# Expert outputs scattered to token order by GpSimd and read back with plain loads, and a re-timed first half of the second sequence's latent attention

## The chip, the cores and the metric

One core of a Trainium2 chip runs the whole kernel. The metric is the device time of one execution in microseconds (us). Before the change the median of three executions is 2420.44 us (2420.27 to 2422.87). Five engines work beside each other: PE (TensorE, matrix products), DVE (VectorE), ACT (ScalarE), POOL (GpSimd) and SP (SyncE, here only an issuer of DMAs). They meet through semaphores.

## The reference

`x` is 2 x 1024 x 256, seen as 2048 rows of 256 floats. Six residual steps follow each other; each reads a layer norm of all that came before:

```python
x = x + 0.5 * moe(norm(x))        # 16 experts, top 2, 256 -> 512 -> 256
x = x + causal_attention(norm(x)) # 16 heads of 16
x = x + 0.5 * moe(norm(x))        # the same weights again
x = x + 0.5 * lora(norm(x))       # base product + 8 routed low-rank pairs, top 2
x = x + latent_attention(norm(x)) # 16 heads, latents of 48 and 64, rotary 64, no mask
x = x + 0.5 * lora(norm(x))
# moe:  out += combine[:, e:e+1] * (silu(x @ W1[e]) @ W2[e])  for 16 experts,
#       combine = softmax of the top 2 router logits at their experts, 0 elsewhere
```

## The kernel before

`X` stays in on-chip memory as 16 token tiles, each 128 rows of 256 floats. Stages run one after the other, each a block in which every engine has its own program; between blocks all engines meet at a barrier.

**Expert stage** (`moe_stage`, run twice). DVE normalizes the token tiles and works out the router's top two. For every token POOL scatters its normalized row twice (L575, 64 indirect DMAs in the two runs) to a slot list in HBM, `slots_in`, grouped by expert; the unused tails of each expert's list are zeroed by plain DMAs from a tile of zeros (L311, on ACT's and SP's queues). Then 48 expert tiles of 128 slots are worked through, two per turn of a loop: SP loads a tile (L328, L329), PE turns it (L539), multiplies it with the first weights (L550), ACT applies SiLU (L473), PE turns and multiplies again (L556, L564), ACT copies the result to `YS` (L477) and stores it in slot order to `slots_out` (L479). `PO` holds for each token the two slots that its outputs went to, and `GH` the two gate weights.

**Reading the outputs** (`ExpertSums`). The stage that follows an expert stage (attention after the first, lora after the second) begins by gathering: per token tile POOL issues two indirect DMAs by `PO` (L218, L219), 32 of them a stage, and DVE adds the two gathered rows, weighted, to `X` and takes the row statistics (L227, L230, L233, L236; `add`). ACT takes the roots (L148), and DVE normalizes (L160). In attention, ACT first writes constants into `att_QT` and `att_KT` (L1038, L1039), then copies and rounds what PE turns and projects (L790, L815; L974, L988). In lora SP also loads the latent stage's big weights ahead (L1236, L1237).

**Latent stage** (`mla_stage`). Two sequences of 1024 rows, each with eight pairs of heads; a pair is 16 steps `s`. Each step has scores on PE (L1752), exponentials on ACT (L1930) and value products on PE (L1761), with sums of exponentials on POOL (L1654). A row's maximum is taken from rough scores (L1733) that PE computes in pieces and DVE reduces (L2062), one pair ahead. In the last pair of the first sequence (`after` in the code) each step also carries a share of the second sequence's front: turning the normalized rows (`xn_transposes`, L1673), the down projection (L1683), the latents' norm (`latent_scales`, L2023 to L2028), their transposes (L1690) and the first rotary projections (L1708, L2042 to L2056). Behind it stand eight turns of the up projection (L1781), each followed by three pieces of the next pair's rough scores.

Of the kernel before, what the change touches and what calls it, by code (L numbers as in the profile page):

```python
# [41 lines left out]
ROWS = NT * P + P  # L42
NB4 = 4
# [20 lines left out]
MOE_STEPS = 55  # L64
# [99 lines left out]
def load_stage(nc, g, dram):  # L164
# [3 lines left out]
    s_z = g.sem("zeros_made")  # L168
    s_zd = g.sem("zero_tile_stored")
    with nc.Block() as block:  # L170
        @block.sync
        def _(sp):
            g.credit(sp)
            sp.dma_start(g.X[:, :, :], dram["x"].rearrange("(t p) d -> p t d", p=P)).then_inc(s_in.handle, 16)
            sp.dma_start(g.C[:, :], dram["const"]).then_inc(s_c.handle, 16)
            sp.wait_ge(s_z.handle, s_z.at(1))
            sp.dma_start(g.XG[NE * ROWS:NE * ROWS + P, :], g.Z[:, :]).then_inc(s_zd.handle, 16)
            sp.wait_ge(s_zd.handle, s_zd.at(16))
            sp.wait_ge(s_c.handle, s_c.at(16))

        @block.vector
        def _(dve):
            dve.memset(g.Z[:, :], 0.0).then_inc(s_z.handle, 1)
# [6 lines left out]
class ExpertSums:  # L190


    NQ = 8
    PER = NT // NQ

    def __init__(self, g, rep):
        S = lambda name, each, **kind: g.sem("moe_" + name, each, rep, **kind)
        self.g = g
        self.s_po, self.s_yd = S("out_rows", 1), S("expert_out_stored", 16 * NTILE)
        self.s_ga = [S(f"rows_gathered{q}", 32 * self.PER, pool_dma=True) for q in range(self.NQ)]  # L200
# [8 lines left out]
    def gather(self, pool, tiles):  # L209

        g, s_second = self.g, self.s_second
        pool.wait_ge(self.s_po.handle, self.s_po.at(1))
        pool.wait_ge(self.s_yd.handle, self.s_yd.at(16 * NTILE))
        for t in tiles:
            if t >= NT // 2:
                pool.wait_ge(s_second.handle, s_second.at(t - NT // 2 + 1))
            s_ga = self.s_ga[t // self.PER]
            pool.indirect_dma_start(self.Y1[:, t, :], None, g.YG, bass.IndirectOffsetOnAxis(g.PO[:, 0, t:t + 1], 0)).then_inc(s_ga.handle, 16)  # L218
            pool.indirect_dma_start(self.Y2[:, t % (NT // 2), :], None, g.YG, bass.IndirectOffsetOnAxis(g.PO[:, 1, t:t + 1], 0)).then_inc(s_ga.handle, 16)  # L219

    def add(self, dve, q, s_mv):

        g = self.g
        tiles = range(q * self.PER, (q + 1) * self.PER)
        dve.wait_ge(self.s_ga[q].handle, self.s_ga[q].at(32 * self.PER))
# [13 lines left out]
def moe_stage(nc, g, dram, rep):  # L239
# [16 lines left out]
    s_pos, s_ei, s_ri, s_po = S("slots", NB4), S("tile_experts", 1), S("tile_rows", 1), S("out_rows", 1)  # L256
    s_tz, s_zt = S("tail_rows", 1), S("tails_zeroed", 16 * NE)
# [6 lines left out]
    s_yd = S("expert_out_stored", 16 * NTILE)  # L264
# [4 lines left out]
    with ExitStack() as ctx:  # L269
# [16 lines left out]
        PI, PO, GH = sb("PI", [P, 2, NT], I32), g.PO, g.GH  # L286
# [5 lines left out]
        CM = sb("CM", [1, NTILE + 2, NE])  # L292
        EF, EC, ES, R1, R2, R3 = (sb(n, [1, NTILE + 2]) for n in ("EF", "EC", "ES", "R1", "R2", "R3"))
# [5 lines left out]
        XS = sb("XS", [P, 2, D])  # L299
# [6 lines left out]
        def zero_tails(engine, first, end):  # L306

            engine.wait_ge(s_tz.handle, s_tz.at(1))
            with engine.Fori(first, end) as e:
                row = engine.value_load(TZ[0:1, bass.ds(e, 1)], min_val=0, max_val=NE * ROWS - P)  # L310
                engine.dma_start(g.XG[bass.ds(row, P), :], g.Z[:, :]).then_inc(s_zt.handle, 16)  # L311

        with nc.Block() as block:
            @block.sync
            def _(sp):
# [4 lines left out]
                for e in range(0, NE, 4):  # L320
                    sp.dma_start(W2[:, e:e + 4], dram["W2"][:, e:e + 4]).then_inc(s_w2.handle, 16)
                zero_tails(sp, 0, NE // 2)
                sp.wait_ge(s_ri.handle, s_ri.at(1))
                sp.wait_ge(s_zt.handle, s_zt.at(16 * NE))
# [8 lines left out]
                with sp.Fori(0, NTILE // 2) as i:  # L333
                    for u in range(2):
                        sp.wait_ge(s_tap.handle, s_tap.at(2 * i + u + 1))
                        load_slots(u, 2 * i + u + 2)

            @block.vector
            def _(dve):
# [11 lines left out]
                def normalized(b):  # L351
                    for t in range(BT * b, BT * (b + 1)):
                        normalize(dve, g, g.XN[:, t, :], t).then_inc(s_xn.handle, 1)

                def routed(b):
# [10 lines left out]
                    then_wait(dve.tensor_copy(IF[:, ts, :], I8[:, ts, :]))  # L366
                    for k in range(2):
# [18 lines left out]
                then_wait(dve.memset(TP[:, :, :], 0.0))  # L386
                for b in range(AHEAD):
# [17 lines left out]
                while dist < NE:  # L405
# [3 lines left out]
                then_wait(dve.tensor_tensor(CM[:, :, :], bcast(TP[0:1, src, pad:], 1, NTILE + 2),  # L409
                                            bcast(g.C[0:1, C_TILE:C_TILE + NTILE + 2], 2, NE), ALU.is_le))  # L410
                then_wait(dve.tensor_reduce(EF[:, :], CM[:, :, :], AX_X, ALU.add))
                then_wait(dve.tensor_scalar(EC[:, :], EF[:, :], float(NE - 1), None, ALU.min))
# [3 lines left out]
                then_wait(dve.tensor_tensor(CM[:, :, :], CM[:, :, :], bcast(TE[0:1, :], 1, NTILE + 2), ALU.mult))  # L416
                then_wait(dve.tensor_reduce(ES[:, :], CM[:, :, :], AX_X, ALU.add))
                then_wait(dve.tensor_tensor(R1[:, :], g.C[0:1, C_TILE:C_TILE + NTILE + 2], ES[:, :], ALU.subtract))
                then_wait(dve.tensor_scalar(R2[:, :], R1[:, :], float(P), None, ALU.mult))
                then_wait(dve.scalar_tensor_tensor(R3[:, :], EF[:, :], float(ROWS), R2[:, :], ALU.mult, ALU.add))  # L420
# [3 lines left out]
                then_wait(dve.scalar_tensor_tensor(MB[:, :], TP[:, src, pad - 1:pad - 1 + NE], float(P), BASE[:, :], ALU.mult, ALU.subtract))  # L424
                then_wait(dve.tensor_tensor(SL[:, :, :], SL[:, :, :], bcast(MB[:, :], 1, NT), ALU.add))
                then_wait(dve.tensor_tensor(PT[:, :, :, :], OH[:, :, :, :], bcast(SL[:, :, :], 1, 2), ALU.mult))
# [1869 lines left out]
```

## Time and profile before

| | us |
|---|---|
| median of three executions | 2420.44 |
| the profiled execution | 2423.66 |
| its span | 2421.9 |
| PE busy | 2018.4 (83%) |
| DVE busy | 1283.6 (53%) |
| POOL busy | 805.5 (33%) |
| ACT busy | 790.0 (33%) |

The span is the time between the first and the last recorded instruction, and all times of rows count from its start. In a row of the order of time, the first number is the start, the second the duration (of all instructions of a merged row together), then engine, line and tiles; the bracket says how long the engine was idle ahead of it and who released it ("issue" and "remote": no releaser on this core's engines is to be seen). In time the stages are: load to 18, first expert stage to 313, attention to 790, second expert stage to 1083, lora to 1240, latent attention to 2340, lora and store to the end. The first expert loop runs from 97 to 311, the second from 868 to 1082.

### The profile page before, as it was taken

The numbers are of one execution on the slowest core, as the hardware profiler recorded it, in microseconds if no ns is written. First come the engines' busy times: TensorE is split into PE (matmuls) and PEld (weight loads), VectorE is DVE, ScalarE is ACT, GpSimd is POOL, SyncE is SP. The second block draws the span as 40 slices with busy tenths as digits, with TensorE's granted clock in tenths as the row PEclk, the third lists the DMA queues.
The fourth block names the chain that finished last, engine by engine and source line by source line (L and its number), as shares of the span: only waits on it lengthen the run. The fifth ranks groups of instructions, "written<-read, shape, count | busy, mean of one in ns | idle before, by whom it ended". The sixth has DMA issues, their size and how long they took to land. (4 is left out here: it accounts for less than half of the span.)

```text
span 2421.9 us, 30646 instructions
## 1 busy us (share of the span) xinstructions
PE 2018.4 (83%) x8676; PEld 1249.4 (52%) x8677; DVE 1283.6 (53%) x2888; ACT 790.0 (33%) x1298; POOL 805.5 (33%) x622
## 2 busy tenths in 40 slices
PE   4499947899898569982669999999969999999996
PEld 4266624555454446652545555555546555555465
DVE  3322245677775512224546666666655666666525
ACT  1022232554545112221223333333422333333312
POOL 2200051221212400005004555555522555555631
PEclk9999967899989579995758999999989999999998
DMA  7311133222320821124032222222031222222101
GB/s 311 137 61 61 61 99 38 35 27 28 52 27 1 345 77 60 59 67 149 6 78 48 53 53 52 52 52 52 5 78 30 50 50 52 52 52 52 29 1 46
DMA packets 85575, 159.78 MB, mean 66 GB/s; under 512 B 14881, under 2 KB 49265, under 8 KB 83185
## 3 DMA queue, kind: packets, MB, share of 16 engines
q1 hardware_dynamic: 63216, 127.25, 20.3%
q0 software_dynamic: 6144, 16.79, 2.1%
q10 hardware_dynamic: 16128, 14.69, 1.7%
q8 instruction: 42, 0.69, 0.1%
q14 instruction: 45, 0.36, 0.1%
HBM read 69.34 MB, written 27.39 MB: 40 GB/s over the span
## 5 line engine op out<-in xcount | busy, mean ns | idle before, releaser
L1654 POOL TENSOR_TENSOR mla_PS<-mla_PS,mla_PT 128x1024 f32<-128x1024 f32 x192 | 458.1, 2386 | 240.9 <-ACT mla_PT L1930 238.4
L2062 DVE TENSOR_REDUCE mla_MXP<-PS 128x1 f32<-128x512 f32 x512 | 342.3, 688 | 232.7 <-PE PS L1733 228.2
L1930 ACT ACTIVATE mla_PT<-PS 128x1024 f32<-128x1024 f32 x256 | 262.6, 1026 | 393.7 <-PE PS L1752 393.3
L1761 PE MATMUL PS<-mla_PT,mla_CN 128*64 128x512 f32 x1024 | 276.1, 618 | 0.2
L1733 PE MATMUL PS<-mla_KH,mla_QH 113*128 113x512 f32 x512 | 213.1, 454 | 35.4 <-DVE mla_MXP L2062 17.9
L446 DVE COPY moe_HT<-PS 128x512 f32<-128x512 f32 x96 | 66.4, 691 | 319.3 <-PE PS L556 313.1
L1752 PE MATMUL PS<-mla_QH,mla_KH 113*128 113x512 f32 x512 | 213.1, 416 | 0.3 <-ACT mla_QH L1917 0.3
L1752 PE MATMUL PS<-mla_QL,mla_KH 113*128 113x512 f32 x512 | 203.9, 398 | 0.0
L1752 PE MATMUL PS<-mla_QH,mla_KL 113*128 113x512 f32 x512 | 202.5, 395 | 0.0
L1733 PEld LDWEIGHTS PS<-mla_KH,mla_QH 113*128 113x128 f32 x512 | 90.6, 193 | 199.8 <-DVE mla_MXP L2062 132.7
L1011 ACT ACTIVATE att_PT<-PS 128x1024 f32<-128x1024 f32 (+1 forms) x192 | 152.5, 812 | 94.3 <-PE PS L851 92.6
L550 PE MATMUL PS<-W,moe_ST 128*128 x384 | 176.8, 604 | 2.7 <-DVE moe_ST L441 2.7
L564 PE MATMUL PS<-moe_W,moe_HT 128*128 x768 | 173.7, 379 | 0.0
L830 PE MATMUL PS<-att_KT,att_QT 128*128 128x512 f32 (+3 forms) x384 | 146.6, 427 | 28.4 <-DVE att_MX L1112 10.1
L1654 POOL TENSOR_TENSOR mla_PS<-mla_PT 128x1024 f32<-128x1024 f32 x32 | 76.3, 2383 | 271.2 <-ACT mla_PT L1930 271.2
L1110 DVE CUSTOM_DVE_ANT_0 PS<-PS,att_SEEN 128x128 f32<-128x128 f32 (+3 forms) x256 | 122.8, 508 | 53.9 <-PE PS L830 51.7
L564 PEld LDWEIGHTS PS<-moe_W,moe_HT 128*128 128x128 f32 x768 | 142.2, 190 | 17.3
L2074 DVE RECIPROCAL PS<-PS 128x128 f32<-128x128 f32 x128 | 108.8, 918 | 69.2 <-PE PS L1768 69.2
L1752 PEld LDWEIGHTS PS<-mla_QH,mla_KH 113*128 113x128 f32 x512 | 97.6, 191 | 76.3 <-issue 30.7
L730 POOL TENSOR_SCALAR_AFFINE_SELECT att_PT<-att_PT 128x256 f32<-128x256 f32 x128 | 52.1, 407 | 252.3 <-ACT att_PT L1011 252.3
L830 PEld LDWEIGHTS PS<-att_KT,att_QT 128*128 128x128 f32 x384 | 75.1, 212 | 107.2 <-DVE att_MX L1112 38.5
L851 PE MATMUL PS<-att_QT,att_KT 128*128 128x512 f32 (+3 forms) x384 | 121.5, 402 | 0.0
(274 smaller groups left out, 3102.0 us busy)
## 6 DMA issues: line engine op xcount, KB each, us to landing
W<-in_W_dram SPq DMA_DIRECT2D x8, 2048.0 KB
moe_W<-in_W_dram SPq DMA_DIRECT2D x8, 2048.0 KB
moe_XS<-slots_in SPq DMA_DIRECT2D x100, 128.0 KB, 2.0
slots_out<-moe_YS ACTq DMA_DIRECT2D x96, 128.0 KB, 1.7
mla_QH<-mla_SH SPq DMA_DIRECT2D x64, 128.0 KB, 2.4
mla_KH<-mla_SH SPq DMA_DIRECT2D x64, 128.0 KB, 2.4
mla_QL<-mla_SL SPq DMA_DIRECT2D x64, 128.0 KB, 2.4
mla_KL<-mla_SL SPq DMA_DIRECT2D x64, 128.0 KB, 2.4
```

The source lines that it names most:

```text
L550: ins = pe.matmul(bank(2 + u)[:, :], ST[:, u, k, :], g.W1[:, experts[u], k, :], start=(k == 0), stop=(k == KD - 1))
L564: ins = pe.matmul(bank(6 + u)[:, 0:D], HT[:, u, k, :], W2[:, experts[u], k, :], start=(k == 0), stop=(k == KF - 1))
L830: ins = pe.matmul(out[:, m, :], QT[:, H % 2, h, i * P:(i + 1) * P], KT[:, H % 2, h // 2, k0:k0 + w], start=(m == 0), stop=(m == len(hs) - 1))
L851: ins = pe.matmul(st_banks(s)[:, hh, c0:HB], KT[:, G % 2, pair, j * P:(j + 1) * P], QT[:, G % 2, 2 * pair + hh, q * HB + c0:(q + 1) * HB], ...
L1011: act.activation(PT[:, kk % 2, 2 * pair:2 * pair + 2, c0:HB], st_banks(s)[:, :, c0:HB], ACT.Exp, scale=SEQ ** -0.5).then_inc(s_p.handle, 1)
L1110: ins = dve.tensor_tensor_reduce(part, part, seen, 1.0, LEAST, ALU.mult, ALU.max, MX[:, q, c, h, t:t + 1])
L1654: pool.tensor_tensor(PS[:, :], PT[:, slot(0), :] if k == 1 else PS[:, :], PT[:, slot(k), :], ALU.add).then_inc(s_ps.handle, 1)
L1733: pe.matmul(bank(piece_bank(n))[:, :], QH[USED, buf, h, tile * P:(tile + 1) * P], KH[USED, buf, h, c * HB:(c + 1) * HB], start=True, stop= ...
L1752: ins = pe.matmul(bank(st_bank(s, h))[:, :], kk[USED, buf, h, ks], qq[USED, buf, h, qs], start=(n == 0), stop=(n == 2))
L1761: ins = pe.matmul(bank(6)[h * DKVL:(h + 1) * DKVL, :], CN[:, b, k, 0:DKVL], PT[:, slot(k), h * HB:(h + 1) * HB], start=(k == 0), stop=(k = ...
L1930: act.activation(PT[:, slot(k), :], banks(st_bank(s, 0), 2)[:, :], ACT.Exp, scale=MLA_SCALE).then_inc(s_p.handle, 1)
L2062: dve.tensor_reduce(MXP[:, n // NPC, c, h, t:t + 1], bank(piece_bank(n))[:, :], AX_X, ALU.max).then_inc(s_mx.handle, 1)
```

## The change

It has three parts.

**Scatter.** Rows of `slots_in` are two floats longer (258, `DX`). They carry the row's destination: its place in token order as a fraction, and the sum of its two experts' numbers, from which DVE finds (`out_row`, two small operations a tile) whether this slot is the token's lower or higher expert and so which half of `slots_out` it belongs to. POOL scatters each of the 48 `YS` tiles to `slots_out` in token order (new L607), each only when the one before has landed, and tells ACT after every second one that the two `YS` buffers are free. ACT no longer stores. `PO` and its five DVE operations are gone; the gate weights are ordered by expert number with seven small ones.

**Plain loads.** The 32 indirect gathers of each following stage become eight plain DMAs of 512 KB on SP's queue, four ahead of the stage's weights and four behind (the last four wait until sums have freed their buffers).

**The latent stage's edge.** In the first sequence's last pair, turning and down projection take two tiles a step for four steps, and not one for eight; the latents' norm and transposes follow at steps 5 to 8, and the first projections are spread over steps 9 to 15. In the up projection the three rough pieces stand between its matrix products and not behind them.

```diff
+DX = D + 2
-MOE_STEPS = 55
+MOE_STEPS = 58
...
-    def gather(self, pool, tiles):
-        pool.wait_ge(self.s_po.handle, self.s_po.at(1))
-        pool.wait_ge(self.s_yd.handle, self.s_yd.at(16 * NTILE))
-        for t in tiles:
...
-            pool.indirect_dma_start(self.Y1[:, t, :], None, g.YG, bass.IndirectOffsetOnAxis(g.PO[:, 0, t:t + 1], 0)).then_inc(s_ga.handle, 16)
-            pool.indirect_dma_start(self.Y2[:, t % (NT // 2), :], None, g.YG, bass.IndirectOffsetOnAxis(g.PO[:, 1, t:t + 1], 0)).then_inc(s_ga.handle, 16)
+    def load(self, sp, groups):
+        rows = lambda k: self.g.YG[k * NT * P:(k + 1) * NT * P, :].rearrange("(p t) d -> p t d", t=NT)
+        sp.wait_ge(self.s_yd.handle, self.s_yd.at(16 * NTILE))
+        for n in groups:
...
+            if n >= 2:
+                sp.wait_ge(self.s_second.handle, self.s_second.at((n - 1) * self.PER))
+            sp.dma_start(self.Y1[:, tiles, :], rows(0)[:, tiles, :]).then_inc(self.s_in[n].handle, 16)
+            sp.dma_start(self.Y2[:, ring, :], rows(1)[:, tiles, :]).then_inc(self.s_in[n].handle, 16)
...
+                def out_row(u, j):
+                    dve.scalar_tensor_tensor(DF[:, bass.ds(j, 1)], XS[:, u, D + 1:DX], E2[:, bass.ds(j, 1)], XS[:, u, D:D + 1], ALU.is_lt, ALU.add).then_inc(s_df.handle, 1)
+                    dve.wait_ge(s_df.handle, s_df.at(j + 1))
+                    dve.tensor_scalar(DI[:, bass.ds(j, 1)], DF[:, bass.ds(j, 1)], float(NT * P), None, ALU.mult).then_inc(s_di.handle, 1)
...
                         act.wait_ge(s_y.handle, s_y.at(2 * i + u + 1))
-                        act.wait_ge(s_yd.handle, s_yd.at(32 * i))
+                        act.wait_ge(s_yf.handle, s_yf.at(i))
                         act.copy(YS[:, u, :], bank(6 + u)[:, 0:D]).then_inc(s_yc.handle, 1)
-                        act.wait_ge(s_yc.handle, s_yc.at(2 * i + u + 1))
-                        act.dma_start(g.YG[bass.ds((2 * i + u) * P, P), :], YS[:, u, :]).then_inc(s_yd.handle, 16)
...
+                for j in range(NTILE):
+                    if j:
+                        pool.wait_ge(s_yd.handle, s_yd.at(16 * j))
+                        if j % 2 == 0:
+                            pool.sem_inc(s_yf.handle, 1)
+                    pool.wait_ge(s_di.handle, s_di.at(j + 1))
+                    pool.wait_ge(s_yc.handle, s_yc.at(j + 1))
+                    pool.indirect_dma_start(g.YG, bass.IndirectOffsetOnAxis(DI[:, j:j + 1], 0), YS[:, j % 2, :], None).then_inc(s_yd.handle, 16)
+                pool.wait_ge(s_yd.handle, s_yd.at(16 * NTILE))
+                pool.sem_inc(s_yf.handle, 1)
...
-    RMS_AT, TURN_AT, FIRST_AT = TB + 1, (TB + 2, TB + 3), (TB + 4, TB + 5)
-    BESIDE = 3
+    FRONT, SCALE_AT, ROWS_AT, TURN_AT = TB // 2, TB // 2 + 1, TB - 1, TB
+    FIRST_AT = {9: ((0, 0), (0, 1)), 11: ((0, 2),), 12: ((1, 1),), 13: ((1, 0),), 15: ((1, 2),)}
+    BESIDE = (2, 5, 7)
...
+                            if k in BESIDE:
+                                rough_scores((b + 1) * NP1, 0, pieces[BESIDE.index(k):BESIDE.index(k) + 1])
```

On ACT, the end of the expert loop's turn (two tiles), in the kernel before:

```order
L476 ISA [waits moe_expert_out_in_psum]
L477 COPY moe_YS<-PS 128x256 [waits moe_expert_out_stored]
L479 ISA [waits moe_expert_out_copied]
L479 DMA slots_out<-moe_YS 128x256
L477 COPY moe_YS<-PS 128x256 [waits moe_expert_out_stored,moe_expert_out_in_psum]
L479 ISA [waits moe_expert_out_copied]
L479 DMA slots_out<-moe_YS 128x256
```

and in the changed kernel, first ACT's turn, with its two copies:

```order
L500 REGISTER_ALU [waits moe_expert_out_in_psum]
L501 COPY moe_YS<-PS 128x256 [waits moe_expert_out_free]
L501 COPY moe_YS<-PS 128x256 [waits moe_expert_out_free,moe_expert_out_in_psum]
L493 REGISTER_ALU
L493 COMPARE_AND_BRANCH
```

The stores have left ACT's program, and the copies wait for a sign that POOL gives after two scatters.

On SP, the start of the attention stage in the kernel before:

```order
L690 DMA att_Wqk<-in_Wqk_dram 128x1024
L691 DMA att_Wv<-in_Wv_dram 128x512
L692 DMA att_Wo<-in_Wo_dram 128x512
L703 DMA att_QT<-att_SH 16x2x1024 [waits att_high_parts,att_filled_by_act]
```

and in the changed kernel (`sums_Y` are the buffers that the outputs are read into, L214 the first half, L215 the second):

```order
L214 DMA sums_Y<-slots_out 128x1024 [waits moe_expert_out_stored]
L215 DMA sums_Y<-slots_out 128x1024
L214 DMA sums_Y<-slots_out 128x1024
L215 DMA sums_Y<-slots_out 128x1024
L724 DMA att_Wqk<-in_Wqk_dram 128x1024
L725 DMA att_Wv<-in_Wv_dram 128x512
L726 DMA att_Wo<-in_Wo_dram 128x512
L214 DMA sums_Y<-slots_out 128x1024 [waits moe_second_added,moe_expert_out_stored]
L215 DMA sums_Y<-slots_out 128x1024
L214 DMA sums_Y<-slots_out 128x1024 [waits moe_second_added]
L215 DMA sums_Y<-slots_out 128x1024
L738 DMA att_QT<-att_SH 16x2x1024 [waits att_high_parts,att_filled_by_act]
```

The row placements of `att_QT` (L738) now stand behind two waits for sums on the same queue.

On PE, the up projection between the two sequences (`mla_UV,mla_LA`) and the rough scores of the second sequence's first pair (`mla_KH,mla_QH`), in the kernel before:

```order
L1781 MATMUL PS<-mla_UV,mla_LA 128x256 [waits mla_latent_out]
L1781 MATMUL PS<-mla_UV,mla_LA 128x256 x7
L1733 MATMUL PS<-mla_KH,mla_QH 128x512 [waits mla_piece_max] x3
L1781 MATMUL PS<-mla_UV,mla_LA 128x256 x8
L1733 MATMUL PS<-mla_KH,mla_QH 128x512 [waits mla_piece_max] x3
```

and in the changed kernel:

```order
L1823 MATMUL PS<-mla_UV,mla_LA 128x256 [waits mla_latent_out]
L1823 MATMUL PS<-mla_UV,mla_LA 128x256 x2
L1775 MATMUL PS<-mla_KH,mla_QH 128x512 [waits mla_piece_max]
L1823 MATMUL PS<-mla_UV,mla_LA 128x256 x3
L1775 MATMUL PS<-mla_KH,mla_QH 128x512 [waits mla_piece_max]
L1823 MATMUL PS<-mla_UV,mla_LA 128x256 x2
L1775 MATMUL PS<-mla_KH,mla_QH 128x512 [waits mla_piece_max]
```

The three pieces that stood together behind eight products now have two or three products between them.

## Rows read from the trace of the kernel before

**Rows 1.** Stretches: start:end, length; PE, PEld, DVE, ACT, POOL busy; clock; DMA share; GB/s.

```profile
97.00:313.00 216.00, 205.42 (x868) 140.48 (x868) 49.92 (x98) 46.55 (x96) 0.00 (x0) 1.00 0.19 59
313.00:420.00 107.00, 59.01 (x167) 35.37 (x167) 54.36 (x161) 35.03 (x50) 39.26 (x45) 0.65 0.32 70
1655.70:1716.70 61.00, 58.30 (x233) 31.75 (x234) 42.34 (x64) 23.68 (x31) 34.96 (x16) 1.00 0.21 52
1713.30:1797.20 83.90, 69.13 (x284) 38.58 (x282) 46.99 (x77) 34.02 (x79) 33.54 (x15) 0.90 0.20 44
1797.20:1849.00 51.80, 39.17 (x164) 30.64 (x165) 24.68 (x44) 2.47 (x5) 2.96 (x3) 0.97 0.11 21
1110.00:1130.00 20.00, 1.04 (x5) 0.79 (x4) 2.48 (x7) 1.05 (x4) 14.10 (x16) 0.59 0.30 85
792.00:815.00 23.00, 18.02 (x83) 16.70 (x84) 10.44 (x60) 6.65 (x17) 4.72 (x5) 0.53 0.99 405
```

**Rows 2.** DMA issues: KB each, us from issue to landing.

```profile
slots_out<-moe_YS ACTq DMA_DIRECT2D x96, 128.0 KB, 1.7
...
att_QT<-att_SH SPq DMA_DIRECT2D x32, 128.0 KB, 4.6
```

**Rows 3.** ACT in order of time, expert loop, the copies of two turns.

```profile
282.86 0.37 ACT L477 COPY moe_YS<-PS 128x256 f32<-128x256 f32 x1 [3.08 <-PE PS L564]
...
291.53 0.37 ACT L477 COPY moe_YS<-PS 128x256 f32<-128x256 f32 x1 [3.08 <-PE PS L564]
```

**Rows 4.** All engines in order of time, from the loop's end into attention.

```profile
308.86 0.37 ACT L477 COPY moe_YS<-PS 128x256 f32<-128x256 f32 x1 [3.08 <-PE PS L564]
...
310.96 0.34 ACTq L479 DMA_DIRECT2D slots_out<-moe_YS  x1
...
313.88 0.21 POOL L709 MEMSET att_MB<- 128x132 f32 x1 [230.94 <-SPq L117]
313.88 0.34 SPq L690 DMA_DIRECT2D att_Wqk<-in_Wqk_dram  x1
```

**Rows 5.** POOL and DVE in order of time, start of attention.

```profile
318.49 0.94 POOL L219 DMA_INDIRECT sums_Y<-slots_out,PO  x1 [0.30 <-issue]
319.74 0.95 POOL L218 DMA_INDIRECT sums_Y<-slots_out,PO  x1 [0.30 <-issue]
...
321.21 0.88 DVE L227 SCALAR_TENSOR_TENSOR X<-sums_Y,GH,X 128x256 f32<-128x256 f32 x2 [6.47 <-DMA sums_Y<-slots_out,PO]
...
326.44 0.88 DVE L227 SCALAR_TENSOR_TENSOR X<-sums_Y,GH,X 128x256 f32<-128x256 f32 x2 [2.68 <-DMA sums_Y<-slots_out,PO]
...
328.69 0.30 DVE L236 BATCH_NORM_AGGREGATE MV<-ST 128x2 f32<-128x6 f32 x2
```

**Rows 6.** ACT in order of time, front of attention.

```profile
324.59 1.28 ACT L148 ACT_TABLE_LOAD   x1
329.02 0.30 ACT L148 ACTIVATE SD<-MV,C 128x4 f32<-128x4 f32 x1 [3.15 <-issue]
...
336.46 0.59 ACT L988 CAST att_SH<-PS 128x512 fp32r<-128x512 f32 x1 [3.58 <-PE PS L815]
...
359.68 0.59 ACT L988 CAST att_SH<-PS 128x512 fp32r<-128x512 f32 x1 [5.95 <-remote]
```

**Rows 7.** DVE in order of time, front of lora.

```profile
1095.54 0.88 DVE L227 SCALAR_TENSOR_TENSOR X<-sums_Y,GH,X 128x256 f32<-128x256 f32 x2 [16.69 <-DMA sums_Y<-slots_out,PO]
...
1130.09 0.18 DVE L154 RECIPROCAL RS<-SD 128x4 f32<-128x4 f32 x1 [12.96 <-ACT SD L148]
...
1138.93 2.20 DVE L160 TENSOR_SCALAR lora_XN<-X,MV,RS 128x256 f32<-128x256 f32 x4
```

**Rows 8.** Issue of the tails' zeros on SP's queue, first expert stage.

```profile
70.15 22.18 SPq L311 DMA_DIRECT2D slots_in<-Z  x8
```

**Rows 9.** PE in order of time, the latent stage's edge.

```profile
1786.92 0.79 PE L1708 MATMUL PS<-mla_CTH,mla_GH 64*128 64x512 f32 x1 [3.71 <-DVE mla_SL L2056]
```

**Rows 10.** PE in order of time, between the sequences.

```profile
1810.79 0.50 PE L1733 MATMUL PS<-mla_KH,mla_QH 113*128 113x512 f32 x1 [1.09 <-DVE mla_MXP L2062]
```

More of the change, by code:

```diff
@@ L190 @@
 class ExpertSums:
-    NQ = 8
-    PER = NT // NQ
+    NG = 4
+    PER = NT // NG
     def __init__(self, g, rep):
@@ L689, in _ @@
                 g.credit(sp)
+                expert.load(sp, range(2))
                 sp.dma_start(WQK[:, :, :, :], dram["Wqk"]).then_inc(s_w.handle, 16)
@@ L692, in _ @@
                 sp.dma_start(WO[:, :, :], dram["Wo"]).then_inc(s_w.handle, 16)
+                expert.load(sp, range(2, 4))
                 sp.wait_ge(s_afill.handle, s_afill.at(4))
@@ L709, in _ @@
                 pool.memset(MB[:, :], 0.0).then_inc(s_fill.handle, 1)
-                expert.gather(pool, range(NT))
                 def later_tiles(b):
@@ L1229, in _ @@
                 g.credit(sp)
+                if sums:
+                    sums.load(sp, range(2))
                 sp.dma_start(WL[:, :, :], dram["Wlora"]).then_inc(s_w.handle, 16)
@@ L1234, in _ @@
                 if ahead:
+                    sums.load(sp, range(2, 4))
                     for dst, name in ((ahead.WKT, "WkT"), (ahead.WQT, "WqT"), (ahead.WVT, "WvT"), (ahead.WOU, "Wout")):
@@ L1250, in _ @@
                     pool.memset(ahead.GK[:, :], 0.0).then_inc(ahead.s_gk.handle, 1)
-                    sums.gather(pool, range(NT))
                 pool.wait_ge(s_hb.handle, s_hb.at(1))
@@ L1563, in mla_stage, with beside @@
         st_bank = lambda s, h: 2 + 2 * (s % 2) + h
+        def beside(i):
+            done = [min(2 + len(BESIDE) * n, NLATE) for n in (i, i + 1)]
+            return range(*done)
         def pairs_of_a_sequence(engine, b, pair):
@@ L1769, in denominators, with first_projections, up_projection @@
                         ins.then_inc(s_dn.handle, 1)
-                    def first_projections(b, half):
-                        if half == 0:
+                    def first_projections(b, parts):
+                        if parts[0] == (0, 0):
                             pe.wait_ge(s_ctl.handle, s_ctl.at(2 * (b + 1)))
-                        for what in ((0, 1, 2), (1, 0, 2))[half]:
+                        for half, what in parts:
                             project(b * NP1, half, what)
-                    def up_projection(b, i):
+                    def up_projection(b, i, pieces=()):
                         if i >= 2:
@@ L1790, in pair @@
                             scores_of(it, buf, s, first and s < 2)
+                            if after:
+                                if 0 < s <= FRONT:
+                                    for j in range(2 * s - 2, 2 * s):
+                                        down_projection(after, j)
+                                if s == TURN_AT:
+                                    for half in range(2):
+                                        latent_transposes(after, half)
+                                if s in FIRST_AT:
+                                    first_projections(after, FIRST_AT[s])
                             if s == 0 and not last:
@@ L1842, in _ @@
                             latent_transposes(0, half)
-                        for half in range(2):
-                            first_projections(0, half)
+                        first_projections(0, ((0, 0), (0, 1), (0, 2), (1, 1), (1, 0), (1, 2)))
                         pe.wait_ge(s_fill.handle, s_fill.at(64))
@@ L1858, in _ @@
                     for i in range(TB):
-                        up_projection(b, i)
-                        if b + 1 < BATCH:
-                            if i == TB - 2:
-                                max_rows(after, 0)
-                            rough_scores(after, 0, range(min(2 + BESIDE * i, NLATE), min(2 + BESIDE * (i + 1), NLATE)))
+                        if b + 1 < BATCH and i == TB - 2:
+                            max_rows(after, 0)
+                        up_projection(b, i, beside(i) if b + 1 < BATCH else ())
                     if b + 1 < BATCH:
@@ L2110, in pair @@
                                 block_max(it, 1)
+                            if after and s == ROWS_AT:
+                                latent_rows(after)
                             maxima(near, todo[:1])
```

186 lines of the change are left out of this document (113 added, 73 removed).

## The prediction

> **What bounds the kernel now.** I read the busy times of stretches first, then each seam in order of time. In the expert loop PE is busy 205.4 of 216 us at full clock, and in a normal pair of the latent stage 58.3 of 61 [rows 1]: there only PE's work counts, and the change takes none of it away. PE starves elsewhere: 59.0 of 107 us at the front of attention at clock 0.65, 69.1 of 83.9 in the last pair of the first sequence, 39.2 of 51.8 between the sequences, and 1.0 of 20 us at the front of lora [rows 1]. In the last, POOL alone works (14.1 us, its indirect gathers), the DMA share is only 0.30, and DVE and ACT wait with "remote" or no releaser in the row. So most of the change's worth must come from these four seams.
>
> **The expert stage, front: +3.** DVE gets two memsets, three small operations and one more a batch: by neighbours of 0.15 to 0.3 us on 16-wide tiles about 0.8 + 4 x 0.17 = 1.5 us ahead of the scatters, in two stages 3 us. The removed slot operations, the new `E2` and the gate weights' seven operations lie beside the zero tails, whose issue alone takes 22.2 us of SP's queue [rows 8]; were that cover gone, they would cost about 2 us a stage. Rows of `slots_in` grow from 1024 to 1032 bytes, 0.8% more: eight tails of 128 KB in 22.2 us are 47 GB/s on this queue, far under the 405 GB/s that the chip moves at 792 to 815 [rows 1, 8]. Bounds: -1 to +12 (a quarter longer tails in both stages).
>
> The Trainium skill ("DMA: Bandwidth & Descriptors", How a descriptor splits into AXI transactions) speaks against this part: a descriptor that doesn't start on a multiple of 256 bytes fetches bytes that it does not use. By it 1032-byte rows cost up to a quarter more beats. Were the tails limited by beats, that would be the +12 above; the row says that they are limited by something four times slower, since two such queues together stay near 95 GB/s, so I take none of it.
>
> **The expert loop: 0, stage ends +4.2 each.** A turn of two tiles lasts 291.53 - 282.86 = 8.67 us [rows 3]. ACT loses two stores, which cost PE nothing. The new chain is on POOL: a scatter waits for ACT's copy and for the scatter before. No row shows a scatter that is waited for. From the nearest, a gather: started at 318.49, its data used at 321.21, so 2.72 us, and 0.30 of issue gap [rows 5]: 3.0 us. A write may land later; with 0.3 + 0.96 of POOL and 1.9 of landing (a plain store lands in 1.7 us, [rows 2]) I take 3.15 us a tile. From above, the slowest placement of the same size lands in 4.6 us, which gives 5.9 us a tile [rows 2]. ACT's first copy of a turn (ends 283.23) must be followed by two scatters before the first copy of the next (291.53): 8.30 us, so the loop is untouched up to 4.15 us a tile. DVE's two operations of 128 x 1 a tile, perhaps 0.15 us each, fall into its idle time: it is busy 50 of 216 us [rows 1]. SP's load also waits for them, behind a wait it had anyway.
>
> At the end the barrier waits for the last two scatters. Before, the last store is issued at 310.96 and the next stage's first DMA at 313.88, that is 2.6 us after the issue's end [rows 4]. Now the scatters start behind the copy that ends at 309.23 and land at 309.23 + 2 x 3.15 = 315.5; the stage starts at about 318.1, 4.2 us later. This is inside the next two terms.
>
> **Attention: -14.** Before, POOL's gathers come every 1.25 us, and four tiles' sums end at 328.99; ACT's root starts at 329.02, the first high part at 336.46, the second at 359.68 [rows 5, 6]. The gap of 23.2 us for the second half is no work: four more tiles are 2 x 2.55 us of sums (326.44 to 328.99 for two). Now SP sends 1 MB first: at 405 GB/s 2.6 us, 0.7 of issue and 1.7 of landing, so it is there at about 323, and four tiles are summed by 328. But ACT's constants and its table, which end at 325.87 [rows 6], move by 4.2 to 330.1 and now bound the root: first high part at 330.1 + 7.4 = 337.5 (+1.1). The second half then follows in about 8.3 us (the first half's 7.4, and sums of two tiles partly in its way): 345.8 and not 359.68, -13.9. The wait of SP's last four loads for sums ends before 345, and the row placements behind them need the high part anyway. Bounds: -17 (the first half loses nothing) and 0 (SP's rows come late behind the loads).
>
> **Lora: -23.** First sums at 1095.54 before; third batch of norms ends at 1138.93 + 2.20 = 1141.1 [rows 7], and the routing starts on it. Now the stage begins at 1083 + 4.2; with the same 4.8 us from start to data 1092, and I take 1094 since small weights share SP's queue. A batch is 5.1 us of sums, 0.7 of root and reciprocal and 2.2 of norms, 8.0 together; three end at 1118.1, which is -23.0. It rests on the stall of 12.96 us at 1130.09 [rows 7] going with the gathers. Bounds: -27 and -2 (the big weights, 4.8 MB, land late and PE waits for them instead).
>
> **The edge: -11.** The last pair lasts 83.9 us with 14.8 of PE idle; a normal pair of 61 us has 2.7 [rows 1]. The surplus is 12.1 us: waits on the latents' norm and on the rotary parts, of which one is 3.71 us at 1786.92 [rows 9], at steps that carry too much at once. Spreading them over seven steps should take nearly all: -11. Two tiles a step in steps 0 to 3 load ACT and DVE more and may cost 1 to 2 us of it. Bounds: -18 (all idle time, and some of the clock's 0.90) and +3 (denser steps run late).
>
> **Up projection: -8.** Seven times PE waits 1.09 us for DVE's maximum of a piece [rows 10]; with two or three products between the pieces DVE's reduction is done: 7 x 1.1 = 7.7. Bounds: -9 and 0.
>
> **Sum.** 3 - 14 - 23 - 11 - 8 = -53 us. The profiled execution took 2423.66 us (span 2421.9); so 2370.7 in such an execution. It lies 3.2 us over the median of the runs, and the forecast against the median is 2420.44 - 53 = 2367.4 us.
>
> **Rivals.**
>
> B: *The engines' stalls are not the gathers'.* For it: in them DVE, ACT and PE all wait for nothing that the trace shows, as an instruction fetch would look. Against: they appear while indirect DMAs run, and at 792 to 815, with a DMA share of 0.99, PE is busy 18 of 23 us [rows 1]. If they stay, lora keeps all but 6 us and attention all but 8: -53 + 17 + 6 = -30, 2390 us.
>
> The Trainium skill ("Runtime: NRT & Kernel Launch", Instruction fetch mechanics) has each engine's instructions refilled over a DMA queue of its own while the previous ones execute. By that rule these stalls are late refills behind other transfers, which plain loads of the same bytes would keep, the result of B; the row at 792 to 815 speaks against it.
>
> C: *The edge gives nothing.* The idle time there moves to the packed steps, because ACT's copies for two tiles and its exponential fill a step of 3.7 us. For it: DVE is already busy 47 of 83.9 us there, ACT 34 [rows 1]. Against: both have room on average. Sum -53 + 11 + 8 = -34, 2386 us.
>
> D: *The scatters bound the expert loop: slower.* If a scatter and its landing take more than 4.15 us, POOL's chain sets the turn: each further us costs 2 x 48 = 96 us. It cancels the gain at 4.15 + 53 / 96 = 4.7 us, and at 5 us gives -53 + 82 = +29, 2449 us. For it: only gathers are in the rows, a write to HBM by 128 row descriptors is not, and the placements of 4.6 us [rows 2] show slow landings beside other traffic. Against: the loop moves 59 GB/s at a DMA share of 0.19 [rows 1].
>
> E: *The parts cancel.* Stage ends, fronts and new waits eat the gain: 2420 us.
>
> **How the numbers follow.** Forecast 62%, B 16%, C 12%, D 8%, E 2%. The predicted time is the forecast's, 2367 us; by its own terms it may lie from 2355 to 2382. The range, 2346 to 2397, takes the low bounds of lora, the edge and attention's together at the one end, B and C with some loss more at the other, and leaves out D. A measurement of this kernel tells about 0.2%, 5 us, from no change: faster 62 + 16 + 12 = 90%, same 2%, slower 8%.
>
> **What would show it.** In the expert loop, POOL's scatters start within a us of ACT's copies, and turns stay at 8.67 us; turns of 10 us would be D. The second stage starts at about 318. Attention's second high part comes some 16 us after the first root and not 31; the front of lora has no stretch of 20 us with all engines still. Such stretches without gathers would be B. The last pair lasts 73 us and not 84; 84 would be C. In the up projection no wait for a piece's maximum is left.

## The result, and the profile after

The changed kernel takes 2384.72 us (median of four, 2382.02 to 2388.34), the kernel before 2420.70; the ratio is 0.9851 (95%: 0.9833 to 0.9868), a gain of 36 us. Run once more beside others it gave 2383.38 us, ratio 0.9841 (0.9825 to 0.9857). I had forecast 2367 with a range of 2346 to 2397. The profiled execution took 2382.02 us with a span of 2380.1, so between the two traces 41.8 us are gone.

The stretches that answer to [rows 1] (expert loop, last pair, between the sequences, front of lora; columns as there):

```profile
99.10:315.30 216.20, 205.63 (x868) 140.61 (x868) 66.20 (x198) 46.51 (x96) 45.28 (x48) 1.00 0.19 59
1691.90:1764.90 73.00, 66.23 (x284) 37.80 (x282) 45.24 (x77) 32.24 (x79) 33.39 (x15) 0.93 0.16 36
1764.90:1808.10 43.20, 38.00 (x168) 31.56 (x165) 25.53 (x45) 2.47 (x5) 2.89 (x3) 0.92 0.24 51
1107.00:1127.00 20.00, 10.40 (x50) 9.70 (x48) 16.29 (x56) 8.65 (x23) 6.39 (x9) 0.74 0.77 296
```

The expert loop is as long as before, with 45 us of GpSimd's scatters and 16 us more of DVE in it. The last pair fell from 83.9 to 73.0 us and the stretch between the sequences from 51.8 to 43.2. In the front of lora there is no still stretch any more: in 20 us PE is busy 10.4 us where it had been 1.0. The two windows lie at different distances from the stage's start. From GpSimd's first instruction of the stage to the end of the third batch of norms it is 31.1 us with 11.8 of PE (1090.25 to 1121.39), and in the kernel before 57.8 us with 11.6 of PE (1083.31 to 1141.13): the same work with the pauses gone. The granted clock of the two 20 us stretches is low (0.59 before, 0.74 now).

The end of the first expert loop and the start of attention, all engines in order of time; it answers to [rows 4]:

```profile
303.59 0.96 POOL L607 DMA_INDIRECT slots_out<-moe_YS,moe_DI  x1 [4.79 <-ACT moe_YS L501]
...
306.45 0.95 POOL L607 DMA_INDIRECT slots_out<-moe_YS,moe_DI  x1 [1.90 <-DMA slots_out<-moe_YS,moe_DI]
...
311.13 0.37 ACT L501 COPY moe_YS<-PS 128x256 f32<-128x256 f32 x1 [3.07 <-PE PS L586]
312.26 0.95 POOL L607 DMA_INDIRECT slots_out<-moe_YS,moe_DI  x1 [4.86 <-ACT moe_YS L501]
312.70 0.37 ACT L501 COPY moe_YS<-PS 128x256 f32<-128x256 f32 x1 [1.20 <-PE PS L586]
314.89 0.95 POOL L607 DMA_INDIRECT slots_out<-moe_YS,moe_DI  x1 [1.67 <-DMA slots_out<-moe_YS,moe_DI]
326.35 3.62 ACT L1072 ACTIVATE att_QT<-C 128x4096 fp32r<-128x4096 f32 x1 [13.27 <-SPq L118]
...
326.37 0.21 POOL L744 MEMSET att_MB<- 128x132 f32 x1 [10.53 <-SPq L118]
326.38 0.33 SPq L214 DMA_DIRECT2D sums_Y<-slots_out  x1
```

Two things are to be seen. From one scatter of a turn to the next it is 2.63 and 2.86 us here (312.26 to 314.89, 303.59 to 306.45). Over all turns it is 2.63 to 2.96 us in the first stage and 2.64 to 3.14 in the second, under the 4.15 at which it would set the turn. And behind the last scatter nothing happens for 10.53 us. Its data has landed 1.7 us after its instruction ended, if it is like the one before; the other 8.9 us hold every engine at the barrier. This is the price that the forecast lacks.

The front of attention on ACT, with the root, the first and the second high part; it answers to [rows 6]:

```profile
337.09 1.28 ACT L149 ACT_TABLE_LOAD   x1
338.38 0.30 ACT L149 ACTIVATE SD<-MV,C 128x4 f32<-128x4 f32 x1
...
345.80 0.58 ACT L1022 CAST att_SH<-PS 128x512 fp32r<-128x512 f32 x1 [3.56 <-PE PS L849]
346.28 0.30 ACT L149 ACTIVATE SD<-MV,C 128x4 f32<-128x4 f32 x1
...
353.65 0.58 ACT L1022 CAST att_SH<-PS 128x512 fp32r<-128x512 f32 x1 [3.87 <-PE PS L849]
```

From root to second high part it is 15.3 us; it had been 30.7. The root waits for the table alone, as forecast. In lora (DVE, the first sums and the third batch's norms, as in [rows 7]) the sums start 6.3 us after the stage and three batches end at 1121.4:

```profile
1096.53 0.88 DVE L223 SCALAR_TENSOR_TENSOR X<-sums_Y,GH,X 128x256 f32<-128x256 f32 x2 [20.39 <-DMA sums_Y<-slots_out]
...
1119.18 2.21 DVE L161 TENSOR_SCALAR lora_XN<-X,MV,RS 128x256 f32<-128x256 f32 x4
```

Between the sequences PE waits for these alone (engine, line, who was waited for, us in all, times, longest). The waits for the maxima of [rows 10] are gone (6.6 us in all, six times), and so is one of 3.6 us for a latent; the 4.3 us for the landing of a placement are new:

```profile
PE PS L1775 <- DMA mla_KL<-mla_SL: 4.3, 1, 4.3
PE PS L1810 <- POOL mla_PS L1696: 0.9, 1, 0.9
```

Both traces side by side, each step counted from the one before it. "Last copy" is the start of ACT's last copy to `YS`, and the next stage starts here with SP's first DMA:

| step | forecast | between the traces | how |
|---|---|---|---|
| two fronts | +3 | +5.7 | last copy 310.42 to 312.70; second stage +3.4 |
| two stage ends | +8.4 | +20.3 | last copy to next stage 3.46 to 13.68, and 3.30 to 13.44 |
| attention, from its start | -18.2 | -19.5 | 477.3 to 457.8 |
| lora, from its start | -27.2 | -27.3 | |
| last pair | -11 | -10.9 | 83.9 to 73.0 |
| up projection | -8 | -8.6 | 51.8 to 43.2 |
| rest | 0 | -1.5 | |
| sum | -53 | -41.8 | |

### The profile page after: what moved, and what is told of

It is laid out like the page before. It is cut to its first block and busy times, and to the rows that moved or that the text cites. A ratio compares the mean times of both kernels' runs of the same rounds, so it can differ in the third digit from the quotient of the medians.

```text
span 2380.1 us, 31116 instructions
## 1 busy us (share of the span) xinstructions
PE 2007.5 (84%) x8676; PEld 1244.9 (52%) x8677; DVE 1316.0 (55%) x3112; ACT 787.6 (33%) x1298; POOL 834.7 (35%) x654
## 5 line engine op out<-in xcount | busy, mean ns | idle before, releaser
L607 POOL DMA_INDIRECT slots_out<-moe_YS,moe_DI x96 | 91.8, 957 | 369.1 <-ACT moe_YS L501 273.5
L864 PE MATMUL PS<-att_KT,att_QT 128*128 128x512 f32 (+3 forms) x384 | 145.5, 423 | 28.7 <-DVE att_MX L1146 10.1
```

The source lines that it names most:

```text
L864: ins = pe.matmul(out[:, m, :], QT[:, H % 2, h, i * P:(i + 1) * P], KT[:, H % 2, h // 2, k0:k0 + w], start=(m == 0), stop=(m == len(hs) - 1))
```

## The experiments

The runs were taken in three groups, and the kernel before, run beside each, took 2427.86 us (the first three runs below and the one with spare gathers in attention and lora), 2420.85 (the run without 46 scatters, the two parts and the first mend) and 2421.30 (the rest). Ratios are to the kernel before of the same group. The changed kernel was not run in the first two groups, so a time from them can't be set against its 2384.72 us to the last few us.

**Whose is the wait at the barrier?** In the kernel before, GpSimd was last at no such barrier: its program of the expert stage had ended 230 us earlier [rows 4]. The first run makes it the last there without any new indirect DMA, by one line in the kernel before.

```diff
                         g.XN[:, t, :], None).then_inc(s_sc.handle, 16)
+                pool.wait_ge(s_yd.handle, s_yd.at(16 * NTILE))
```

> The kernel before, with one wait more: GpSimd's program of the expert stage ends with a wait for the landing of ACT's last plain store, so that GpSimd is the last engine at the barrier though its last indirect DMA was issued 230 us earlier. In the changed kernel the next stage starts 10.5 us after the last scatter's instruction ends, where I had forecast 4. Theory F (leaving the block is slow for GpSimd whenever it is last, whatever it did before: its code at the jump's end isn't there yet): the stages start 7 to 9 us later than in the kernel before (attention at about 322), the time rises by 14 to 18 us, to 2435. Theory G (the delay belongs to an indirect DMA that was just issued and must be drained): the landing adds 1 to 2 us a stage, attention starts at 315 to 316, the time is 2423.

2437.85 us, ratio 1.0036 (1.0026 to 1.0046). The last store is issued at 310.33, and attention starts so:

```profile
317.27 0.21 POOL L710 MEMSET att_MB<- 128x132 f32 x1 [235.08 <-SPq L117]
```

That is 6.9 us after the issue, where the kernel before has 2.9 (310.96 to 313.88); in the second stage it is 5.4 and 1.4. So 4.0 us a stage: more than a landing of 1.7 us, and less than the 7 to 9 of theory F. Neither fits. From the landing (310.33 + 1.7) GpSimd takes 5.2 us to let the next stage begin, and 3.7 in the second. The next run leaves the changed kernel as it is, but lets ACT and not GpSimd wait for the last landing.

```diff
                         act.copy(YS[:, u, :], bank(6 + u)[:, 0:D]).then_inc(s_yc.handle, 1)
+                act.wait_ge(s_yd.handle, s_yd.at(16 * NTILE))
...
-                pool.wait_ge(s_yd.handle, s_yd.at(16 * NTILE))
                 pool.sem_inc(s_yf.handle, 1)
```

> The changed kernel, but ACT and not GpSimd waits for the landing of the last scatter at the end of the expert stage; GpSimd's program ends when it has issued that scatter. Theory F (GpSimd's own way out of the block is slow): its exit starts 1.5 to 2 us earlier in both stages, so attention starts at about 324.5 and the time falls by 3 to 4 us, to 2381. Theory G (the delay counts from the landing, a drain of the queue): no change, 2385.

2380.16 us, ratio 0.9800 (0.9783 to 0.9816). Attention starts 9.04 us after the last scatter's end and not 10.53, lora 7.92 and not 9.44:

```profile
315.06 0.96 POOL L608 DMA_INDIRECT slots_out<-moe_YS,moe_DI  x1 [1.67 <-DMA slots_out<-moe_YS,moe_DI]
325.06 0.21 POOL L744 MEMSET att_MB<- 128x132 f32 x1 [9.04 <-SPq L118]
```

1.5 of the 1.67 us of landing are gone from the gap in both stages: the time runs from the end of GpSimd's program and not from the landing, as F says. Its size isn't explained. The third run writes the 48 scatters as a loop.

```diff
-                for j in range(NTILE):
-                    ...
+                with pool.Fori(0, NTILE // 2) as i:
+                    for u in range(2):
+                        pool.wait_ge(s_di.handle, s_di.at(2 * i + u + 1))
+                        pool.tensor_copy(DX2[:, u:u + 1], DI[:, bass.ds(2 * i + u, 1)]).then_inc(s_dx.handle, 1)
+                        ...
+                        pool.indirect_dma_start(g.YG, bass.IndirectOffsetOnAxis(DX2[:, u:u + 1], 0), YS[:, u, :], None).then_inc(s_yd.handle, 16)
+                        pool.wait_ge(s_yd.handle, s_yd.at(16 * (2 * i + u + 1)))
+                    pool.sem_inc(s_yf.handle, 1)
```

> The changed kernel, but GpSimd's 48 scatters are a loop of 24 turns with two scatters each (the index column is copied to a fixed place by GpSimd first, one small operation a tile) and not 48 written out one after the other. Theory F with its cause in the length of straight code: the way out is as short as for the other engines, attention starts at 318 to 320 instead of 326, and the time falls by 12 to 16 us, to about 2370. Theory G (a drain after an indirect DMA): the start stays at 326 and the time at 2385 to 2387.

2383.03 us, ratio 0.9820 (0.9803 to 0.9836). The gap is as it was (10.71 and 9.61 us, for 10.53 and 9.44), so the length of the 48 scatters' straight code is not the cause:

```profile
317.32 0.98 POOL L609 DMA_INDIRECT slots_out<-moe_YS,moe_DX  x1 [0.78 <-POOL moe_DX L605]
...
329.01 0.21 POOL L746 MEMSET att_MB<- 128x132 f32 x1 [10.71 <-SPq L118]
```

**Does the price grow with the number of indirect DMAs?** One kernel leaves out 46 of each stage's 48 scatters (the signs to ACT stay), one adds 32 spare gathers to each stage, ahead of the loop.

```diff
+                    if j < NTILE - 2:
+                        ...
+                        continue
```

> The changed kernel with only the last two of the 48 scatters (46 tiles' outputs are left out, the rows of slots_out are zeroed at the stage's front instead). It tells whether GpSimd's way out of the block depends on how many indirect DMAs it issued in the loop. If it has a fixed price: still 9 to 10.5 us from the last scatter to the next stage. If the price is for scatters that pile up: under 6 us. The 32 scatters of the stage's front are in both.

2387.89 us in one run. The gap is 6.78 and 5.19 us, and not 10.53 and 9.44 (the stage's front has 33 zeroing DMAs more in it, so the time of the run isn't compared):

```profile
321.35 0.95 POOL L616 DMA_INDIRECT slots_out<-moe_YS,moe_DI  x1 [1.67 <-DMA slots_out<-moe_YS,moe_DI]
329.09 0.21 POOL L753 MEMSET att_MB<- 128x132 f32 x1 [6.78 <-SPq L118]
```

```diff
+                pool.tensor_copy(JI[:, :], g.C[:, C_CNT:C_CNT + 1]).then_inc(s_ji.handle, 1)
+                pool.wait_ge(s_ji.handle, s_ji.at(1))
+                for t in range(32):
+                    pool.indirect_dma_start(JU[:, t, :], None, dram["x"].rearrange("r (a b) -> (r a) b", b=16), bass.IndirectOffsetOnAxis(JI[:, 0:1], 0)).then_inc(s_ju.handle, 16)
+                pool.wait_ge(s_ju.handle, s_ju.at(512))
                 for j in range(NTILE):
```

> The changed kernel with 32 spare indirect gathers of 64-byte pieces in each expert stage, between the front's 32 scatters and the loop's 48. From the last landing to the next stage's first instruction the runs so far show, with GpSimd last: 5.2 and 3.6 us behind 32 indirect DMAs in the block (first and second stage), 5.1 and 3.5 behind 34, 8.85 and 7.75 behind 80. Theory H (leaving the block costs GpSimd about 0.08 us for each indirect DMA of the block, beside some 2.5 us): with 112 it is 11.4 and 10.4, so the first instruction of attention comes 13.1 us after the last scatter's end and not 10.5, that of lora 12.1 and not 9.4. Rival (only the scatters of the loop count, or the price has an upper bound): 10.5 and 9.4 as in the changed kernel.

The gap is 13.15 and 12.03 us, where theory H said 13.1 and 12.1 ahead of the run (the time, 2465.17 us in one run, has the loop's late start in it):

```profile
352.80 0.96 POOL L614 DMA_INDIRECT slots_out<-moe_YS,moe_DI  x1 [1.68 <-DMA slots_out<-moe_YS,moe_DI]
366.91 0.21 POOL L751 MEMSET att_MB<- 128x132 f32 x1 [13.15 <-SPq L118]
...
1159.53 0.96 POOL L614 DMA_INDIRECT slots_out<-moe_YS,moe_DI  x1 [1.67 <-DMA slots_out<-moe_YS,moe_DI]
1172.51 1.05 POOL L1294 MEMSET mla_GK<- 64x1152 f32 x1 [12.03 <-SPq L118]
```

From the last landing to the next stage, by the number of indirect DMAs in the block (gap less 1.68 of landing; the first row from the plain store):

| indirect DMAs | first stage | second stage |
|---|---|---|
| 32 (old) | 5.2 | 3.7 |
| 34 | 5.1 | 3.5 |
| 80 | 8.85 | 7.76 |
| 112 | 11.5 | 10.35 |

The slope is (11.5 - 5.1) / 78 = 0.082 and (10.35 - 3.5) / 78 = 0.088 us for each; what is left over is 2.3 to 2.6 us in the first stage and 0.5 to 0.9 in the second. It makes no difference whether they were issued 230 us ago or just now (32 and 34), nor whether they moved 128 KB or 8 KB (80 and 112).

**What was it in the gathers?** The changed kernel with 32 spare gathers in attention and in lora, 64 bytes a row, used by nobody:

```diff
+    def spare(self, pool):
...
+        for t in range(32):
+            pool.indirect_dma_start(self.JU[:, t % 32, :], None, g.YG.rearrange("r (a b) -> (r a) b", b=16), bass.IndirectOffsetOnAxis(self.JI[:, 0:1], 0)).then_inc(self.s_ju.handle, 16)
...
                 pool.memset(MB[:, :], 0.0).then_inc(s_fill.handle, 1)
+                expert.spare(pool)
...
+                    sums.spare(pool)
+                    pool.wait_ge(sums.s_ju.handle, sums.s_ju.at(16 * 32))
```

> The changed kernel, with 32 spare indirect gathers on GpSimd at the start of attention and of lora, where the kernel before had its own; they fetch 64-byte pieces that nobody uses (1/16 of the bytes, the same number of descriptors), and the plain loads stay. Theory A (running indirect gathers hold all engines up): the stretches with every engine still come back; in lora the third batch of norms ends 15 to 20 us later than in the changed kernel, attention's second high part 5 to 8 us later, the time is about 2405 to 2412. Theory B (what helped is that the data come sooner by plain loads): DVE's and ACT's front stays as it is in the changed kernel; only GpSimd's own bias additions in lora start later, which costs under 6 us: 2385 to 2391.

2420.62 us, ratio to the kernel before 0.9975 (0.9965 to 0.9986): most of the gain is gone again. The changed kernel with the scatters as a loop, run in the same group, took 2383.03, so the spare gathers cost some 38 us. The rows are ACT's in attention, and ACT's, DVE's and PE's in lora:

```profile
352.97 0.37 ACT L1018 COPY att_XT<-PS 128x256 f32<-128x256 f32 x1 [4.16 <-remote]
357.87 0.37 ACT L1018 COPY att_XT<-PS 128x256 f32<-128x256 f32 x1 [4.53 <-remote]
362.83 0.37 ACT L1018 COPY att_XT<-PS 128x256 f32<-128x256 f32 x1 [4.58 <-issue]
372.66 0.59 ACT L1032 CAST att_SH<-PS 128x512 fp32r<-128x512 f32 x1 [9.46 <-remote]
...
1131.90 0.27 ACT L1391 COPY lora_ML<-PS 128x136 f32<-128x136 f32 x1 [5.52 <-issue]
1136.83 0.37 ACT L1397 COPY lora_XT<-PS 128x256 f32<-128x256 f32 x1 [4.65 <-issue]
1146.69 0.27 ACT L1391 COPY lora_ML<-PS 128x136 f32<-128x136 f32 x1 [9.48 <-issue]
1146.86 0.30 ACT L149 ACTIVATE SD<-MV,C 128x4 f32<-128x4 f32 x1
...
1147.19 0.18 DVE L155 RECIPROCAL RS<-SD 128x4 f32<-128x4 f32 x1 [18.02 <-issue]
...
1147.87 0.69 PE L1328 MATMUL PS<-C,lora_XN 128*128 128x128 f32 x2 [19.91 <-issue]
```

The stall is back with all its marks: ACT's copies 5 us apart, DVE still for 18 us and PE for 19.9. In lora the engine that is held up is ACT. PE's last product ahead of the pause ends at 1127.96 and DVE's last statistics at 1129.17, but ACT's three copies come only at 1131.90, 1136.83 and 1146.69; behind them stands the root that DVE waits for, and PE waits for DVE's norms. In attention DVE is held up too: a sum of its own (L235) starts at 359.27, 2.5 us after the step that it needs. The stall doesn't end with the gathers. GpSimd's last one ends at 1152.1 in lora, 5.4 us behind ACT's third copy, and at 368.2 in attention, 4.4 us ahead of ACT's second high part. Counted from each stage's start, attention's second high part comes 18.5 us later than in the changed kernel (45.8 and 27.3), lora's third root 21.6 us later (50.0 and 28.4). Theory A holds, and is stronger than I expected (20 to 27 us in all): the bytes are 1/16, so it comes from the indirect gathers' running and not from how much they move. B falls. How a gather on GpSimd holds ACT and DVE up is not shown.

**Do the parts add up?**

The kernel before, with the changed kernel's `mla_stage` alone:

> The kernel before with the latent stage's edge alone (two tiles a step, spread projections, rough pieces between the up projection's products). Theory A (the edge's gain is its own, as forecast -11 and -8): 19 to 20 us less than the kernel before, ratio 0.992. Rival C (the edge gives nothing by itself, and what the changed kernel shows there comes with the earlier stages): no change, ratio 1.000.

2400.09 us (2399.76 to 2400.50), ratio 0.9916 (0.9900 to 0.9933): -20.3 us by the ratio. The edge's gain is its own, and rival C falls.

And the other way round, the changed kernel with `mla_stage` as it was before:

> The changed kernel with the edge as it was before: scatter and plain loads alone. If the parts add up: -42 + 20 = 22 us less than the kernel before in the spans (fronts +5.5, stage ends +20, attention -19.5, lora -27), ratio 0.991. If the edge needs the other part or the other way round, this run and the one with the edge alone don't add up to the changed kernel's 0.985.

2406.45 us, ratio 0.9945 (0.9928 to 0.9961): -13.3 us by the ratio, where I expected -22 from the spans. In its profile attention starts as in the changed kernel, 10.54 us after the last scatter. 20.3 + 13.3 = 33.6 us against 36.0 of both: within the intervals the parts add up. They add up in the spans too: 2398.0 and 2403.2 are 23.9 and 18.7 us under the 2421.9 of the kernel before, 42.6 together and 41.8 in the changed kernel. So of the 8.7 us missing from the expectation, 3.3 are missing in the span as well, and the rest is the difference between spans and the other executions.

**Mends.**

In the first, GpSimd's first work in attention (`finish`) is the last two scatters of the first expert stage:

```diff
+    def finish(self, pool):
...
+        for j in range(NTILE - 2, NTILE):
+            pool.wait_ge(self.s_yd.handle, self.s_yd.at(16 * j))
+            pool.indirect_dma_start(g.YG, bass.IndirectOffsetOnAxis(g.DI2[:, j % 2:j % 2 + 1], 0), g.YS[:, j % 2, :], None).then_inc(self.s_yd.handle, 16)
+        pool.wait_ge(self.s_yd.handle, self.s_yd.at(16 * NTILE))
...
-                for j in range(NTILE):
+                last = NTILE - 2 if rep == 0 else NTILE
+                for j in range(last):
```

> The changed kernel, but after the first expert stage GpSimd leaves the block when the 46th scatter has landed and issues the last two as its first work in the attention stage (the second expert stage is left as it is). Theory G (leaving the block costs GpSimd some 9 us from the end of its program when indirect DMAs were just issued): the way out runs beside the last two tiles' products, attention starts at about 318.5 and not 326.4, the sums' first data come 4 us earlier, and since ACT's constants bound the front, the whole comes 6 to 8 us earlier: about 2378. Theory F' (the time runs from the last landing of any scatter, or the barrier itself takes 9 us): attention still starts at 326, the time is the changed kernel's or 3 us over it, 2385 to 2388.

2377.60 us, ratio 0.9827 (0.9805 to 0.9849). GpSimd leaves the block while the last two tiles are still multiplied, and the stage starts at 318.4:

```profile
308.98 0.18 POOL L623 COPY DI<-moe_DI 128x2 int32<-128x2 int32 x1 [1.71 <-DMA slots_out<-YS,moe_DI]
...
312.65 0.37 ACT L510 COPY YS<-PS 128x256 f32<-128x256 f32 x1 [1.20 <-PE PS L595]
318.44 0.96 POOL L210 DMA_INDIRECT slots_out<-YS,DI  x1 [9.28 <-SPq L118]
```

9.28 us of it are there still, from the end of GpSimd's work to the stage's start, but 3.9 of them lie ahead of the end of ACT's last copy. With ACT's wait (the second run's edit) in the second stage beside it:

> Both mends together: the last two scatters of the first expert stage moved into attention, and ACT waiting for the last landing of the second. From the single runs: -7 and -1.5 us against the changed kernel: about 2376, ratio to the kernel before 0.982, and faster than the changed kernel run beside it.

> The changed kernel once more, on the chip of the version with both mends. Ratio to the kernel before 0.985 as measured first.

2374.54 us (2373.51 to 2375.14), ratio 0.9802 (0.9787 to 0.9816), beside 2383.38 us and 0.9841 for the changed kernel in the same group: 8.8 us faster than the changed kernel, and the fastest version run here.

## Why the prediction was right or wrong

The direction, the range and the mechanism were right in the main; the size was 53 and came out as 36 (41.8 between the profiled executions).

- *Expert loop: 0.* Right. The turn stays at 8.67 us (302.46 to 311.13), since a scatter's cycle is 2.63 to 3.14 us. My 3.15 lies at its upper end, and 4.15 was not reached. Rival D did not come true: a scatter lands 1.67 to 2.19 us after its instruction ends.
- *Stage ends: +4.2 each.* This is the step that failed: 10.2 and 10.1 us, 11.9 us too little in all. I had taken the way through the barrier (2.6 us) from a stage that ACT ended last [rows 4], and given it to GpSimd. For GpSimd, after 80 indirect DMAs, it is 8.85 and 7.76 us from the landing. The trace of before could not show it, since GpSimd's leave-taking lay under 230 us of waiting. A bound was missing here: the one term of a new last engine had no row, and I priced it at one value.
- *Fronts: +3.* Measured +2.3 and +3.4. The first is 0.8 over my 1.5; the second's other 1.9 us were not tested. In its trace the third batch's indices come 17.8 us after the second's (812.18 to 829.94) and in the kernel before 13.1 (820.02 to 833.09); in between, beside GpSimd's scatters, one of ACT's copies stands 8.8 us with "remote". The zeros' issue on SP took 21.5 us and not 22.2: the 1032-byte rows cost nothing there, and the bound of a quarter longer tails was far off.
- *Attention: -14, lora: -23.* Without the stage ends -18.2 and -27.2 forecast, -19.5 and -27.3 measured. That the stalls are the gathers' is shown by the spare gathers, which bring them back at 1/16 of the bytes; rival B had this reversed. The Trainium skill ("Runtime: NRT & Kernel Launch", Instruction fetch mechanics) has an engine's sequencer fetch its next instructions over a DMA queue of its own while it executes the current ones. No run here shows whether the engines waited for such a fetch, held up by the gathers. Plain loads at a DMA share of 0.77 in lora's front leave PE working 10.4 of 20 us, so other transfers alone don't cause the stall.
- *Edge: -11, up projection: -8.* Measured -10.9 and -8.6, and -20.3 alone (ratio 0.9916). The totals are closer than their parts. I had put all of the 11 on PE's idle time. That fell by 8.0 us (14.8 to 6.8), and the other 2.9 are PE's busy time, 69.1 to 66.2 us for the same 284 products at a granted clock of 0.93 instead of 0.90. Of the waits, the 7.2 us on the rotary parts [rows 9] have gone and 2.2 of 4.1 for the latents' norm are left. A packed step lasts as long as two of the old: the second and third exponentials lie 7.1 us apart (1697.24 and 1704.32), where they had lain 3.5. In the up projection the waits for maxima were 6.6 us and not 7.7, and that the sum came out at 8.6 is in part luck: 3.6 us of wait for a latent went too, and 4.3 for a placement came.
- *The rest*: of the 17 us between forecast and median, 11.2 are in the trace (stage ends +11.9, fronts +2.7, the others -3.4). The remaining 6 are the difference between one pair of profiled executions and the medians: the changed kernel's four executions spread over 6 us, and the one before change that was profiled lies 3 us above its median.

## What to carry to other kernels

When a change makes another engine the last one at a barrier, its way out of the block becomes visible and has to be priced for that engine; a row in which it waited tells nothing of it. GpSimd's way out grew here with the indirect DMAs of the block, so end its program early and give its last ones to the next stage, or let another engine wait for their landing. Indirect gathers beside straight-line work on the other engines can cost more in the others' stalls than in their own time: move an indirection to a loop that doesn't feel it, and read back plainly.

## What the runs showed of the hardware

- From the end of GpSimd's program to its first instruction of the next stage it took about 2.4 us and 0.082 for each indirect DMA issued in that block in the first stage, and about 0.6 us and 0.088 for each in the second, for 32 to 112 of them. An experiment with 112, priced ahead, came within 0.1 us. Whether it is paid by the DMA or by the row (all have 128 rows) was not tried.
- Beside 32 indirect gathers of 128 rows of 64 bytes, three copies of ACT in lora came after 5.5, 4.7 and 9.5 us of idleness with their inputs there. It began 14 us after the first gather's start (1112.09 to 1126.4) and ended 5.4 us before the last one's end. DVE and PE stood still for 18.0 and 19.9 us behind it. In attention it lasted beyond the last gather, by 4.4 us. In the expert loops 48 scatters, one in flight at a time, left the 216 us of the loop and PE's 205.6 us of work in it as they were. Whether that is because they are spaced or because the engines run in a loop there is open.
- A scatter of 128 rows of 1 KB to memory landed 1.67 to 2.19 us after the end of its instruction of 0.96 us (96 scatters); the gather of [rows 5] took 1.8 us from the end of its instruction to the use of its data.
